# The smallest expert passes with samples stationary and weights moving, and their ReLU results transposed by TensorE

## The reference

```python
s0 = relu(x @ swi[0]) @ swo[0];  s1 = relu(x @ swi[1]) @ swo[1]
h  = relu(einsum('bsd,bdf->bsf', x, wi[type_label]))
eo = einsum('bsf,bfd->bsd', h, wo[type_label])
w  = softmax(relu(concat([eo[:,0], s0[:,0], s1[:,0]]) @ g1) @ g2)
x  = x + eo*w[:,0] + s0*w[:,1] + s1*w[:,2]
x  = x + zX*laplace_x(x) + zY*laplace_y(x) + zR*x*(1 - x)
```

## Time and profile before

| | us |
|---|---|
| median of three runs | 1144.71 (1143.75 to 1145.2) |
| the profiled execution | 1144.29, of which the span of the trace is 1142.8 |
| TensorE busy | 1134.5 (99% of the span) |
| weight loads busy | 969.8 (85%) |
| VectorE / ScalarE / GpSimd busy | 676.4 / 455.4 / 78.8 |
| DMA, mean | 98 GB/s, most of it in the first third of the span |

### The profile page before, as it was taken

The page is one execution under the profiler, slowest core; times in us unless marked ns, Lnnn a source line. Parts: engine busy times, 40 slices in busy tenths (PEclk is TensorE's granted clock), DMA queues, the critical chain, the costliest instruction groups (busy, mean ns, idle before and its releaser), DMA issues.

```text
span 1142.8 us, 16856 instructions
## 1 busy us (share of the span) xinstructions
PE 1134.5 (99%) x6068; PEld 969.8 (85%) x6068; DVE 676.4 (59%) x1031; ACT 455.4 (40%) x806; POOL 78.8 (7%) x123
## 2 busy tenths in 40 slices
PE   8999999999999999999999999999999999999998
PEld 7888888888888888888888888888888888888888
DVE  5665666666666644646646655665565465555556
ACT  3454556555555522333333323323323233233333
POOL 1111212112111100000000000000000000000001
PEclk9999999999999999999999999999999999999999
DMA  8555656646665414023022021131230230221300
GB/s 267 176 166 167 187 173 199 189 146 180 192 185 166 140 39 109 19 65 84 15 70 68 26 75 31 61 76 25 60 84 17 67 84 13 72 52 42 75 29 24
DMA packets 111253, 111.84 MB, mean 98 GB/s; under 512 B 78441, under 2 KB 87234, under 8 KB 111170
## 3 DMA queue, kind: packets, MB, share of 16 engines
q1 hardware_dynamic: 96706, 59.58, 19.3%
q0 software_dynamic: 13952, 50.60, 14.6%
q10 hardware_dynamic: 512, 0.59, 0.2%
HBM read 89.40 MB, written 17.04 MB: 93 GB/s over the span
## 4 chain that ended last, share of the span: by engine, by line
PE 98%; DMA 1%; issue 0%; DVE 0%; ACT 0%; SPq 0%; DVEq 0%; ACTq 0%
PE acc L923 31%; PE hbank L896 16%; PE hbank L895 16%; PE hbank L897 16%; PE acc L924 16%; PE tbank L849 1%; PE acc L909 1%; DMA rw<-in_L_cond_swi 0%; PE hbank L874 0%; PE hbank L875 0%; PE tbank L844 0%; PE tbank L857 0%; PE tbank L850 0%; PE acc L934 0%; PE acc L935 0%
## 5 line engine op out<-in xcount | busy, mean ns | idle before, releaser
L583 DVE SCALAR_TENSOR_TENSOR hl<-hbank,hh 128x512 fp32r<-128x512 f32 (+2 forms) x440 | 275.4, 627 | 424.5 <-ACT hh L1034 424.0
L1034 ACT ACTIVATE hh<-hbank 128x512 fp32r<-128x512 f32 (+2 forms) x440 | 240.2, 546 | 587.6 <-PE hbank L897 584.6
L923 PE MATMUL acc<-swo,hh 128*128 128x512 f32 x992 | 359.3, 396 | 0.0
L924 PE MATMUL acc<-swo,hl 128*128 128x256 f32 x992 | 277.8, 280 | 0.0
L923 PEld LDWEIGHTS acc<-swo,hh 128*128 128x128 f32 x992 | 186.3, 188 | 43.7
L895 PE MATMUL hbank<-xh,swh 128*128 128x512 f32 (+1 forms) x528 | 205.3, 389 | 0.0
L896 PE MATMUL hbank<-xl,swh 128*128 128x512 f32 (+1 forms) x528 | 205.0, 388 | 0.0
L897 PE MATMUL hbank<-xh,swl 128*128 128x512 f32 (+1 forms) x528 | 202.1, 383 | 0.0
L924 PEld LDWEIGHTS acc<-swo,hl 128*128 128x128 f32 x992 | 187.1, 189 | 9.6
L923 PE MATMUL acc<-ewo,hh 128*128 128x512 f32 x528 | 194.6, 398 | 0.3
L924 PE MATMUL acc<-ewo,hl 128*128 128x256 f32 x528 | 148.0, 280 | 0.0
(11 more groups left out here) (194 smaller groups left out, 892.9 us busy)
## 6 DMA issues: line engine op xcount, KB each, us to landing
rw<-in_L_cond_wi POOLq DMA_DIRECT2D x44, 512.0 KB, 4.4
rw<-in_L_cond_wo POOLq DMA_DIRECT2D x44, 512.0 KB, 4.8
eo_scratch<-eo SPq DMA_DIRECT2D x128, 64.0 KB, 2.6
xs<-in_x SPq DMA_DIRECT2D x16, 512.0 KB, 4.4
rw<-in_x SPq DMA_DIRECT2D x256, 32.0 KB, 2.2
ei<-eo_scratch SPq DMA_DIRECT2D x16, 512.0 KB, 5.5
xs<-in_x SPq DMA_DIRECT2D x125, 64.0 KB, 3.1
out<-ot SPq DMA_DIRECT2D x15, 512.0 KB, 6.3
```

The source lines that it names most:

```text
L583: e.scalar_tensor_tensor(h_slot(HL, g), bank[:, 0:w], 0.0, h_slot(HH, g).bitcast(F32), ALU.max, ALU.subtract).then_inc(h_lo, 1)
L923: e.matmul(acc[j][:, 0:2 * D], HH[:, g % NH, js], woc[:, c, :], start=(c == 0), stop=False)
L924: m = e.matmul(acc[j][:, D:2 * D], HL[:, g % NH, js], woc[:, c, 0:D], start=False, stop=last)
L1034: e.activation(h_slot(HH, g), hbank[g % HRING][:, 0:w], ACT.Relu).then_inc(h_hi, 1)
```

## The change

The change treats the four tiny passes in another way and leaves big and small passes as they are.

A tiny pass has four chunks instead of eight. In chunks 0 and 1 (`upright_product`) the 128 sample rows are stationary and the weights move, 512 columns wide: six matmuls give the hidden values of all 128 rows for 512 features. ScalarE takes ReLU of them in plain float32 into `HU`, which lies in the same memory as `HH`; VectorE does nothing for them. In chunks 2 and 3 (`turn_hidden`) TensorE transposes `HU`, four blocks of 128 x 128 into one bank; ScalarE and VectorE split the bank into `HH` and `HL`, 512 columns wide. Two chunks later, that is in chunks 0 and 1 of the next pass, `tiny_product` does the second product of four feature blocks at once, all into `acc[0]`.

The transposes of the tile that follows the tiny one move from chunks 3 and 6 of the tiny pass to chunk 7 of the pass ahead of it and chunk 0 of the tiny pass. The weight cuts around a tiny pass move: those for the tiny unit stand one to three chunks earlier, the next unit's piece 0 at chunk 7 of the pass ahead and piece 2 at chunk 0 of the tiny pass; pieces 1 and 3 stay in chunks 0 and 1 of the pass behind. A cut no longer waits for the end of the pass that used its target, but for that piece's last reader (`last_reader`).

```diff
 def tile_parts(n, c):
...
+    if tiny(n):
+        return [(tile, 1)] if c == 0 else []
+    if tiny(n + 1) and c == 7:
+        return [(tile + 1, 0)]
...
 def unit_cuts(n, c):
...
-        at = {4: 0, 5: 2, 6: 1, 7: 3} if n == 2 else {2: 0, 4: 2} if UNITS[n - 2][1] == 2 else {2: 0, 4: 2, 5: 1, 7: 3}
+        if tiny(n):
+            at = {0: (n + 1, 2)}
+        elif tiny(n + 1):
+
+            at = {1: (n + 1, 0), 2: (n + 1, 2), 4: (n + 1, 1), 5: (n + 1, 3), 7: (n + 2, 0)}
...
+            def upright_product(g):
...
+                fs = slice(c * 512, (c + 1) * 512)
+                if c == 0:
+                    e.wait_ge(t_free, T_AT[tile_last(tile)])
+                e.wait_ge(*cut_done(weight_set(n), c))
+                for k in range(2):
+                    e.matmul(bank[:], xh[k], wh[:, k, fs], start=(k == 0), stop=False)
+                    e.matmul(bank[:], xh[k], wl[:, k, fs], start=False, stop=False)
+                    i = e.matmul(bank[:], xl[k], wh[:, k, fs], start=False, stop=(k == 1))
+                i.then_inc(h_prod, 1)
+
+            def turn_hidden(g):
+                bank, place = hbank[g % HRING], (g - 2) % NH
+                e.wait_ge(h_hi, g - 2 + 1 - 2 * NC)
+                for q in range(3):
+                    e.transpose(bank[:, q * 128:(q + 1) * 128], HU[:, place, q * 128:(q + 1) * 128], ident[:])
+                e.transpose(bank[:, 384:512], HU[:, place, 384:512], ident[:]).then_inc(h_prod, 1)
+
+            def tiny_product(g):
...
+                e.wait_ge(*low_done(g))
+                e.wait_ge(*cut_done(weight_set(n), c))
+                if c == 2:
+                    e.wait_ge(acc_free, acc_before(n, 0))
+                for q in range(4):
+                    hs, f = slice(q * 128, (q + 1) * 128), (c - 2) * 4 + q
+                    e.matmul(acc[0][:, 0:2 * D], HH[:, g % NH, hs], woc[:, f, :], start=(f == 0), stop=False)
+                    m = e.matmul(acc[0][:, D:2 * D], HL[:, g % NH, hs], woc[:, f, 0:D], start=False, stop=(f == NC - 1))
+                m.then_inc(h_used if c == 2 else acc_done, 1)
...
                     if ws >= 4:
-                        e.wait_ge(acc_done, ACC[ws - 2, blocks(ws - 2) - 1])
+
+                        g = last_reader(ws - 2, p)
+                        if p < 2:
+                            e.wait_ge(h_prod, g + 1)
+                        else:
+                            e.wait_ge(*products_done(g))
```

More of the change, by code:

```diff
@@ L45, with tiny, chunks, upright @@
 HALVES = {NP - 2: (0, 2), NP - 1: (1, 3)}
-CHUNKS = [(n, c) for n in range(NP) for c in range(NC)]
-G = len(CHUNKS)
+def tiny(n):
+    return PASSES[n][0] == EXP and UNITS[PASSES[n][1]][1] == 2
+def chunks(n):
+    return 4 if tiny(n) else NC
+CHUNKS = [(n, c) for n in range(NP) for c in range(chunks(n))]
+AT_CHUNK = {k: g for g, k in enumerate(CHUNKS)}
+END = [AT_CHUNK[n, chunks(n) - 1] + 1 for n in range(NP)]
+G = len(CHUNKS)
+def upright(g):
+    return tiny(CHUNKS[g][0]) and CHUNKS[g][1] < 2
+def is_last(g):
+    n, c = CHUNKS[g]
+    return c == chunks(n) - 1
 def width(n):
@@ L168, with last_reader @@
 CUT_LO = {k: i + 1 for i, k in enumerate(k for n, c in CHUNKS for k in low_parts_at(n, c))}
+USED = {g: sum(not upright(i) and not is_last(i) for i in range(g + 1)) for g in range(G)}
+LOWS = {g: sum(not upright(i) for i in range(EARLY, g + 1)) for g in range(G)}
+def last_reader(n, p):
+    return AT_CHUNK[n, p if tiny(n) else 3 + p % 2 * 4]
 def slots_of(u):
@@ L199, in cond_resid_program @@
         SWO = [sb(f"swo{i}", [128, NC, 2 * D], F32R) for i in range(2)]
+        with ExitStack() as upright_room:
+            HU = sb("hu", [128, NH, 512], F32, upright_room)
         HH = sb("hh", [128, NH, 512], F32R)
@@ L354, in piece_src, with products_done, h_width, bank_free @@
             return a[:, :, p * 512:(p + 1) * 512] if p < 2 else b[:, (p - 2) * 4:(p - 1) * 4, :]
+        def products_done(g):
+            n, c = CHUNKS[g]
+            if is_last(g):
+                return acc_done, ACC[n, list(block_order(n))[-1]]
+            return h_used, USED[g]
         def h_free(g):
[L357 to L360, removed]
+            return (h_prod, g + 3) if upright(g) else products_done(g)
+        def h_width(g):
+            return 512 if tiny(CHUNKS[g][0]) else width(CHUNKS[g][0])
         def h_slot(a, g):
             n, c = CHUNKS[g]
-            return a[:, c // 2, c % 2 * 256:(c % 2 + 1) * 256] if n == NP - 1 else a[:, g % NH, 0:width(n)]
+            return a[:, c // 2, c % 2 * 256:(c % 2 + 1) * 256] if n == NP - 1 else a[:, g % NH, 0:h_width(g)]
         def low_done(g):
-            return (h_early, g + 1) if g < EARLY else (h_lo, g + 1 - EARLY)
+            return (h_early, g + 1) if g < EARLY else (h_lo, LOWS[g])
+        def bank_free(g):
+            return (h_hi, g + 1 - 2 * NC) if upright(g) else low_done(g)
         def tile_bank(tile, k):
@@ L572, in hidden_low @@
                 n, c = CHUNKS[g]
-                w = width(n)
+                w = h_width(g)
                 bank = hbank[g % HRING]
-                if g < EARLY:
+                if g < EARLY or upright(g):
                     return
@@ L754, in _ @@
                     own_slot()
-                if g >= LAG and CHUNKS[g - LAG][1] == NC - 1 and CHUNKS[g - LAG][0] < NP - 2 and g - LAG != 2 * NC - 1:
+                if g < G and tiny(n):
+                    for ws, p in low_parts_at(n, c):
+                        cut_low(ws, p)
+                if g >= LAG and is_last(g - LAG) and CHUNKS[g - LAG][0] < NP - 2 and g - LAG != 2 * NC - 1:
                     evacuate(CHUNKS[g - LAG][0])
@@ L769, in _ @@
                         add_x_last(0)
-                if g < G:
+                if g < G and not tiny(n):
                     for ws, p in low_parts_at(n, c):
@@ L875, in first_product @@
                     e.matmul(bank[:, 0:128], rw[:, 1, cs], XF[:, 1, :], start=False, stop=True).then_inc(h_prod, 1)
+                    return
+                if tiny(n):
+                    if c < 2:
+                        upright_product(g)
+                    else:
+                        turn_hidden(g)
                     return
@@ L898, in first_product @@
                 i.then_inc(h_prod, 1)
+            def upright_product(g):
+                n, c = CHUNKS[g]
+                wh, wl, _ = weights(n)
+                tile, bank = tile_of(n), hbank[g % HRING]
+                xh, xl = ([unit_cols(a[tile % 2])[:, k, 0:128] for k in range(2)] for a in (XH, XL))
+                fs = slice(c * 512, (c + 1) * 512)
[14 more added lines that the diff above has]
+            def tiny_product(g):
+                n, c = CHUNKS[g]
+                woc = weights(n)[2]
+                e.wait_ge(*low_done(g))
[7 more added lines that the diff above has]
+                m.then_inc(h_used if c == 2 else acc_done, 1)
             def second_product(g):
@@ L902, in second_product @@
                 last = c == NC - 1
+                if tiny(n):
+                    if c >= 2:
+                        tiny_product(g)
+                    return
                 e.wait_ge(*low_done(g))
@@ L1033, in hidden_high @@
                     e.wait_ge(*h_free(g - NH if n < NP - 1 else G - 2 * NC + 4 + c // 2))
-                e.activation(h_slot(HH, g), hbank[g % HRING][:, 0:w], ACT.Relu).then_inc(h_hi, 1)
+                e.activation(h_slot(HU if upright(g) else HH, g), hbank[g % HRING][:, 0:w], ACT.Relu).then_inc(h_hi, 1)
             def evacuate(n):
```

20 lines of the change are left out of this document (12 added, 8 removed).

## The result

The changed kernel takes 1137.55 us (median of four, 1136.62 to 1138.1), the kernel before on the same chip 1144.43 us: ratio 0.9939, 95% interval 0.9922 to 0.9956, 6.9 us faster. A second reading of the change, on another occasion, gave 0.9940.

The account below looks back on a forecast made before the run. TensorE, busy 99% of the span, was taken as the bound; each of four tiny units goes from 19.07 to 17.30 us, 7.1 us in all: 1144.29 - 7.1 = 1137.2, plus 0.4 gives 1137.6 us; 8-in-10 range 1135.8 to 1140.8.

Parts of the forecast that it names:

- stretch: TensorE's time from the big pass's last chunk to the next pass's first output product: 19.07 us before, 17.30 forecast.
- The low end of the forecast's own range: Whole-kernel time of 1136.1 us, with no wait at all and 4 x 2.04 us gained.
- The wide forms for the narrow ones: Tiny unit's first product on TensorE: samples stationary, weights moving 512 columns wide, 0.233 us a matmul; narrow form wastes half.
- The 11 wide groups: TensorE's wide product groups in one tiny unit's sequence, 1.395 us each, 15.35 us together.
- The turns: TensorE's transposes of `hu`, four per turn at 0.09 us: two turns and 0.08 on the matmul behind, 0.80 us.
- The added wait at `tbank`: Ahead of the next tile's transposes part 1, TensorE waits for VectorE's low part: 0.27 us, bounds 0 and 0.6.
- The wait that goes: Output product of the pass behind no longer waits for VectorE's evacuation of the tiny unit: 0.25 us a unit.
- The margin at the tiny output product: `hl` ready at 11.71 us, when TensorE reaches the first tiny output product: margin nil, wait put at 0.
- The rival of a late turned chunk: Evacuation copies on ScalarE delay `hh`; TensorE loses 0.9 us a unit, 3.6 in all: 1141 us; chance 0.20.
- Splits at nothing: Earlier weight splits on ScalarE and VectorE around a tiny pass: same number, cost nothing beside products.
- the later readers' waits: Waits ahead of weight splits for a piece's last reader, costed at nothing.
- The other rule weighed: Trainium skill: weight loads overlap matmuls only when row groups differ; 28 fewer loads would give 3.9 us more a unit.

## Why the prediction was right, step by step

The forecast was 1137.6 us, with a stretch of 17.30 us; measured were 1137.55 and 17.44 (mean of four). That the times agree to 0.05 is partly luck. The stretch gained 1.64 a unit and not 1.77, and the forecast added 0.4 because the median of before lay that much above its profiled execution; the change's median lies 0.55 below its own. The low end of the forecast's own range, 1136.1, leaves these 0.4 out.

- **The wide forms for the narrow ones.** Right: samples stationary and weights moving goes at 0.23, as taken. The 11 wide groups take 1.40 each, not 1.395: 0.05 more.
- **The turns** were put at 0.80 for two with the matmul behind; measured 0.88 (74.39 to 75.18, and 0.09 on the matmul behind). A turn with another one behind it takes 0.44, and 0.36 only with a wide matmul behind it, which then takes 0.09 longer. My sum took 0.36 for both and the longer matmul once. The doubled turns gave 0.11 a transpose, not 0.09.
- **The added wait at `tbank`** was put at 0.27; idle 0.24, and the transposes behind it 0.06 more. Its cause was right, as moving the transposes showed. Of the chain's links one was off by more than 0.05: from VectorE's end to TensorE's start it is 0.05 (68.21 to 68.26), and I had put 0.15.
- **The wait that goes** (0.25 at the evacuated `acc`) went, and with it the 0.07 that its next matmul lost, outside the stretch: the three pieces between the units are shorter by 0.08 to 0.11 each.
- **The margin at the tiny output product** was put at nil and is 0.3. The chain on ScalarE and VectorE came as forecast: counted from the stretch's start, `hh` at 10.23 (10.24 forecast) and `hl` done at 11.55 (11.56). Half of the 0.3 is the 0.15 that I had put between VectorE's end and TensorE's start; the other half is TensorE, which gets there at 11.86 and not at 11.71, late by its turns and by the matmuls' 1.40. The rival of a late turned chunk fell because each evacuation copy waits for its own block, as forecast.
- **Splits at nothing.** Right for their places. At the early places it holds only because the wait ahead of them was loosened. In the forecast that edit stood among "the later readers' waits", at nothing; the run with the old wait is 19.7 us slower, and I had not asked for this price.
- **What I missed** is the border to the shared passes. There a chain that was in time by 0.7 us came 0.46 us late, since one issue on SyncE's queue took 1.1 us longer. I had looked for late things only inside the stretches, and had put SyncE's queue at nothing.

By the two profiled executions: 6.54 in the stretches and 0.29 between them, less 0.39 for a later start of the first stretch (the first expert matmul of the kernel came at 24.09 against 23.69, ahead of anything that the change touches) and 0.24 behind the last stretch, the border wait among it, is 6.2, the difference of the spans. The medians differ by 6.9; the start alone varies by more than that difference between executions.

**The rules weighed.** The trace of the doubled turns decides on the transposes: 0.11 us each in a row, clock 1.00 behind sixteen of them. The Trainium skill's 275 ns (page TensorE: Matmul & The Clock Gate, Part 4) is again the row's length. Its sentence that transposes don't hold up the clock is neither confirmed nor refuted by these sixteen; they did not bring it down here. The other rule weighed, by which the weight loads saved would be worth 3.9 us more a unit, is not borne out: in the first stretch loads are busy 14.6 us and matmuls 17.4 of 17.46, so they overlap as before, and the whole gain is 1.6.

## What to carry to other kernels

Where TensorE is the bound, compare the forms by their starts, per column: if a narrow moving side costs the same at 64, 128 and 256 columns, make the small operand stationary and move the wide one, and pay for the turned result with transposes at their pace. Sum TensorE's row in one stretch and check the other engines' chain against it at each point where the distance between producer and user shrinks. Then look at what the earlier arrival meets outside the stretch, and at any wait in an in-order engine that an earlier place puts ahead of its releaser.

## What the runs showed of the hardware that I had not expected

- In the run with the old wait TensorE stands 2.27 us ahead of a turn in each of four units, in a kernel that is busy otherwise. In three of them the granted clock then fell to about 0.50 (the 1.2 GHz level; wide matmuls 0.43 apart in place of 0.23), in the third unit it stayed at 1.00 with the same waits. What tells them apart wasn't found. It cost 0.3 us in one unit and nothing in the others, since `hl` came last there. In the change, whose longest idle time in a stretch is 0.24, it did not happen.
- A matmul of 64 moving columns with a fresh stationary operand starts no sooner after its neighbour than one of 128 columns (0.11 us) or of 256 (0.12).
- One of 16 equal DMA issues on SyncE's queue takes 1.3 to 1.7 us instead of 0.61 in the two traces of the change and in all six of variants that left these loads in their place; none does in the kernel before, in its variant with 64 columns, and where the loads go out earlier. What sets it wasn't found.
- The four transposes straight after the wait at `tbank` take 0.42 us, 0.06 more than without it.
